# Eleven one-hot lookups in every block, and gathers tied to matmul steps, in a recommendation model's top network

## The chip, the cores and the metric

The kernel runs on one core of a Trainium2 chip. The metric is device time of one execution in microseconds; the median of three runs of the kernel before is 498.77 us (496.91 to 505.03). TensorE (PE) multiplies, VectorE (DVE) and ScalarE (ACT) copy and round, GpSimd (POOL) issues the row gathers, SyncE (SP) issues most other transfers.

## The reference, cut to what matters

```python
e = stack([tbl_f[ids[:, f]] for f in range(26)], axis=1)        # 2048 x 26 x 128, fp32
all_emb = concatenate([bottom[:, None, :], e], axis=1)          # 27 features of 128
gram = einsum('bfd,bgd->bfg', all_emb, all_emb)
h = concatenate([gram[:, triu_i, triu_j], bottom], axis=1)      # 351 + 128
h = maximum(h @ W_top1 + b_top1, 0)                             # 479 -> 512
h = maximum(h @ W_top2 + b_top2, 0)                             # 512 -> 256
y = h @ W_top3                                                  # 256 -> 1
```

Eleven of the 26 tables have 1000 rows (`ONEHOT`). The others have 1250 to 125000.

## The kernel before, in words

The 2048 samples are 16 tiles of 128, in 4 blocks of 4 tiles. An embedding row reaches the matmuls in one of two ways.

**Gather.** POOL issues one indirect transfer for each tile and gathered table (L591): 128 rows land in `rows`, with samples on the partitions. The gathers of a tile come in groups of up to four (`groups_of`), a group fills one of 10 places of the ring `rows`, and POOL waits before a group only until the group ten before it has been transposed. PE transposes a group in one *turn* (`turn(t, g)`, L637, one transpose for each gather), and ACT copies it from PSUM to `features` (L741).

**One-hot lookup.** A *visit* v looks one table up for two blocks (`VISITS`, `lookup(v)`): the table's 1000 rows lie as 8 chunks of 125, and for each chunk and block PE multiplies a high and a low part of the table with a one-hot matrix of 512 samples (L624, L625): 8 x 2 x 2 = 32 matmuls. DVE builds six of the eight one-hot columns (L899) and the low part in two halves (L893), ACT builds columns 2 and 5 (L769, L772) and the high part. Results for block 0 stay in `looked`; those for blocks 1 to 3 go through `staged` to the DRAM tensor `parked` and return, a block at a time, in one transfer of 2.5 to 2.8 MB (`load_looked`, SP, L511). ACT's `place(t)` copies a tile's share into `features`.

`LOOKUPS = (10, 10, 11, 11)` says how many of the eleven small tables are looked up in each block; the rest are gathered. So there are 10 + 11 = 21 visits, and 16 gathers for each tile of blocks 0 and 1 and 15 for each tile of blocks 2 and 3: 8 x 16 + 8 x 15 = 248 gathers in 64 groups (tiles 0 to 7: 4, 4, 4, 4; tiles 8 to 15: 4, 4, 4, 3).

**What follows.** `gram_chunk(t, j)` (L655, four for each tile, 32 matmuls in the trace) makes the products of 32 samples. They go through `products` and `square` in DRAM (SP, `store_products` after a tile's last gram) to `pairs`, and the layers follow for each part of a block (`layer1(part, m)`, `layer2`, `output`).

**The order.** All engines follow one list, `ORDER`, made by `order()`. It keeps a planned time `now` in tenths of a microsecond (`LENGTH`: a lookup 80, a gram 10, a turn 5, a layer-1 column 30, a layer 2 58) and a planned time `gathered` up to which gathers have landed, 13 for each gather. A turn is put in as soon as its rows are planned to be there, no more than four tiles ahead of the grams, and no later than its tile's first gram. PE takes the list strictly in order. Ten visits come first, then block 0's grams with seven visits between them, then block 1's with four; in blocks 2 and 3 there are none. The last stretch of interest here is that of tiles 9 to 13: in the kernel before, `... gram(9,1) turn(12,0) gram(9,2) gram(9,3) gram(10,0) gram(10,1) turn(12,1) layer1(1,0) gram(10,2) layer1(1,1) turn(12,2) gram(10,3) turn(12,3) layer1(1,2) gram(11,0) layer1(1,3) turn(13,0) ...`. SP reaches `load_looked(3)`, the return of block 3's lookups, right after it has stored the products of tile 9, that is after gram(9,3).

Of the kernel before, what the change touches and what calls it, by code (L numbers as in the profile page):

```python
# [18 lines left out]


ONEHOT = [3, 4, 9, 13, 14, 17, 20, 21, 22, 23, 24]
LOOKUPS = (10, 10, 11, 11)
ALWAYS, MOST = min(LOOKUPS), max(LOOKUPS)
ONEHOT_ROWS = 1000
CHUNKS = 8
# [53 lines left out]
TILE_CHUNKS = RUN // CHUNK_GROUPS  # L79
# [27 lines left out]
def groups_of(t):  # L107

    n = TABLES - LOOKUPS[t // BLOCK_TILES]
    return [min(GROUP, n - g) for g in range(0, n, GROUP)]  # L110
# [3 lines left out]
LENGTH = {"lookup": 80, "gram": 10, "layer1": 30, "layer2": 58, "output": 6, "turn": 5, "place": 0, "bottom": 0}  # L114
GATHER_LENGTH = 13
GATHER_START = -20

VISITS = [(i, (b, b + 1)) for b in range(0, BLOCKS, VISIT_BLOCKS) for i in range(LOOKUPS[b])]
FIRST_LATER = LOOKUPS[0]
AMONG = (7, MOST - 7, 0, 0)
# [56 lines left out]
def order():  # L180

    turns = [("turn", t, g) for t in range(TILES) for g in range(len(groups_of(t)))]
    steps, now, gathered = [], 0, GATHER_START
    grams = 0

    def turn():
        nonlocal now, gathered
        step = turns.pop(0)
        gathered += groups_of(step[1])[step[2]] * GATHER_LENGTH
        now = max(now, gathered) + LENGTH["turn"]  # L190
        steps.append(step)

    def rows_are_there():
        t, g = turns[0][1:]
        return t < grams // TILE_CHUNKS + FEATURE_RING and gathered + groups_of(t)[g] * GATHER_LENGTH <= now

    for step in products_and_others():
        if LENGTH[step[0]] and turns and rows_are_there():
            turn()
        while step[0] == "gram" and turns and turns[0][1] <= step[1]:  # L200
            turn()
        steps.append(step)
        now += LENGTH[step[0]]
        grams += step[0] == "gram"
    return steps


ORDER = order()


def accumulations():
# [17 lines left out]
def visited(v):  # L229

    return FILL["lookup", v, VISITS[v][1][-1]] + 1
# [37 lines left out]
def dlrm_tower(nc, xT, ids, onehot_ids, gathered, onehot_tables, w1, b1, w2, b2, w3, square,  # L269
               parked, out):  # L270
    with ExitStack() as ctx:
# [53 lines left out]
        gram = psum("gram", [P, GRAM_RING, BANK])  # L325
# [24 lines left out]
        grammed = sem("grammed")  # L350
        onehot_used = sem("onehot_used")
        accumulated = sem("accumulated")
# [89 lines left out]
        def at_least(eng, semaphore, count):  # L442
            if count > 0:
                eng.wait_ge(semaphore, count)
# [128 lines left out]
        def _(pool):  # L573
# [6 lines left out]
            pool.wait_ge(identity_zero, 1)  # L580
            pool.affine_select(out=identity[:], in_=identity[:], compare_op=ALU.not_equal, fill=1.0,
                               base=0, pattern=[[-1, P]], channel_multiplier=1).then_inc(identity_ready, 1)
            for t in range(TILES):
                if t in (0, FIRST_TILES):
                    pool.wait_ge(index_landed[0 if t == 0 else 1], 16)
                for g, size in enumerate(groups_of(t)):
                    n = groups_before(t) + g
                    at_least(pool, transposed, n - ROWS_RING + 1)
                    for i in range(size):
                        f = GROUP * g + i  # L590
                        pool.indirect_dma_start(  # L591
                            out=rows[:, n % ROWS_RING, i, :], out_offset=None, in_=gathered[f],
                            in_offset=bass.IndirectOffsetOnAxis(ap=index[:, t, f:f + 1], axis=0),
                        ).then_inc(rows_landed[n % ROWS_RING], 16)
# [140 lines left out]
        def _(act):  # L735
# [60 lines left out]
            def place_first(last):  # L796

                at = LOOKED_AT[VISITS[last][0]]
                act.wait_ge(acc_out, FILL["lookup", last - 1, 0] + 1)
                copy_place(0, MOST - LOOKUPS[0], at).then_inc(placed_ahead, 1)  # L800
                looked_up(last, 0)
# [260 lines left out]
```

## Time and profile before

| | us |
|---|---|
| median of three runs | 498.77 |
| lowest, highest | 496.91, 505.03 |
| span of the profiled execution | 370.7 |
| busy in it: PE, DVE, ACT, POOL | 343.2, 236.3, 230.8, 257.2 |

The span runs from the first to the last instruction of the program on the engines. The median is 128 us above it; that part lies around the program, and nothing in the trace shows it. Matmuls overlap, so the pitch from one start to the next is what a matmul costs, not its duration.

### The profile page before, as it was taken

To read this page: it belongs to the slowest core of one execution; us is meant where nothing else is said; L and a number is where in the kernel's file an instruction comes from. 1 tells how busy PE (TensorE), PEld (TensorE's weight loads), DVE (VectorE), ACT (ScalarE), POOL (GpSimd) and SP (SyncE) were. 2 spreads that over 40 slices of the span, in tenths; PEclk is the share of its full clock that TensorE was granted. 3 is DMA by queue.
4 is the path that set the end of the run, shared out by engine and by line. 5 is a ranking of instruction groups with operands and counts; after the bars stand their busy time and mean duration, and the time that the engine had idled before them with its cause. 6 is when DMAs were issued, how large, how long until landed. Compare 5 with 4: busy or idle time off the path is not lost.

```text
span 370.7 us, 8525 instructions
## 1 busy us (share of the span) xinstructions
PE 343.2 (93%) x3422; PEld 282.3 (76%) x3422; DVE 236.3 (64%) x312; ACT 230.8 (62%) x298; POOL 257.2 (69%) x261
## 2 busy tenths in 40 slices
PE   6899999999699999999999999997977996899996
PEld 5688888887587778788788877776866785677886
DVE  2999999999497769798789945313340332522452
ACT  2699989888497896499997833447321473223222
POOL 5777878777777777777877877777777777770010
PEclk9699999999699999999999999999896999899999
DMA  6977687665957789988767629534593425323200
GB/s 174 249 217 211 194 248 222 190 198 163 319 112 251 205 242 341 287 235 252 230 156 245 191 77 347 176 96 114 152 366 99 115 74 146 97 52 85 66 20 2
DMA packets 48391, 66.86 MB, mean 180 GB/s; under 512 B 15861, under 2 KB 34847, under 8 KB 47840
## 3 DMA queue, kind: packets, MB, share of 16 engines
q1 hardware_dynamic: 40024, 49.32, 43.9%
q0 software_dynamic: 8064, 16.31, 16.7%
q10 hardware_dynamic: 264, 0.69, 0.6%
q8 instruction: 27, 0.44, 0.5%
q14 instruction: 12, 0.10, 0.1%
HBM read 52.36 MB, written 13.93 MB: 179 GB/s over the span
## 4 chain that ended last, share of the span: by engine, by line
PE 69%; POOL 10%; DMA 6%; ACT 5%; issue 5%; DVE 3%; SPq 1%; ACTq 0%; DVEq 0%
PE acc L624 21%; PE acc L625 21%; POOL rows L591 10%; PE gram L655 9%; PE turned L637 6%; PE acc L660 4%; PE acc L661 4%; PE acc L662 4%; DMA rows<-in_tbl,index 2%; DMA wanted<-in_onehot_ids 2%; DVE onehot L899 2%; ACT features L741 1%; ACT staged L823 1%; ACT h L769 1%; DMA square<-products 1%
## 5 line engine op out<-in xcount | busy, mean ns | idle before, releaser
L591 POOL DMA_INDIRECT rows<-in_tbl,index x248 | 253.9, 1024 | 77.7 <-issue 74.4
L899 DVE TENSOR_SCALAR onehot<-wanted,row_number 125x1029 fp32r<-125x1029 int32 (+3 forms) x137 | 151.0, 1150 | 19.6 <-PE acc L625 13.3
L624 PE MATMUL acc<-onehot,table_hi 125*128 125x512 f32 x336 | 136.6, 407 | 3.1 <-DVE table_lo L893 3.1
L625 PE MATMUL acc<-onehot,table_lo 125*128 125x512 f32 x288 | 115.7, 402 | 0.0
L624 PEld LDWEIGHTS acc<-onehot,table_hi 125*128 125x128 f32 x336 | 64.7, 193 | 17.8 <-DVE table_lo L893 3.3
L655 PEld LDWEIGHTS gram<-features 128*54 128x54 f32 x2048 | 60.6, 136 | 17.6 <-issue 14.6
L655 PE MATMUL gram<-features 128*54 128x52 f32 x2048 | 67.5, 222 | 6.0 <-DVE features L925 3.0
L625 PEld LDWEIGHTS acc<-onehot,table_lo 125*128 125x128 f32 x288 | 55.7, 194 | 12.4
L769 ACT ACTIVATE h<-wanted,row_number 125x1029 f32<-125x1029 int32 x42 | 48.8, 1163 | 23.4 <-PE acc L625 20.3
L637 PE MATMUL turned<-identity,rows 128*128 128x128 f32 x248 | 41.8, 294 | 9.9 <-DMA rows<-in_tbl,index 8.1
L772 ACT ACTIVATE onehot<-h,row_number 125x1029 fp32r<-125x1029 f32 x42 | 48.6, 1157 | 1.4
L741 ACT COPY features<-turned 128x512 f32<-128x512 f32 x64 | 39.3, 628 | 16.2 <-PE turned L637 15.4
L637 PEld LDWEIGHTS turned<-identity,rows 128*128 128x128 f32 x248 | 29.8, 148 | 17.1 <-DMA rows<-in_tbl,index 9.5
L816 ACT ACTIVATE h<-acc,b_sb 128x512 f32<-128x512 f32 (+1 forms) x20 | 12.1, 604 | 47.7 <-PE acc L662 47.7
L729 DVE COPY products<-gram 117x416 f32<-117x416 f32 x32 | 18.8, 587 | 30.1 <-PE gram L655 23.7
L961 DVE CAST onehot<-h 128x512 fp32r<-128x512 f32 (+1 forms) x20 | 8.0, 399 | 45.0 <-ACT h L816 41.9
L893 DVE TENSOR_TENSOR table_lo<-table_raw,table_hi 125x512 fp32r<-125x512 f32 x36 | 24.6, 682 | 1.7 <-ACT table_hi L761 1.7
L660 PE MATMUL acc<-pairs_hi,w_hi 128*128 128x512 f32 (+1 forms) x60 | 22.3, 371 | 3.2 <-DVE pairs_lo L956 3.0
L729 ACT COPY products<-gram 117x416 f32<-117x416 f32 x32 | 16.1, 504 | 14.6 <-PE gram L655 14.1
L761 ACT CAST table_hi<-table_raw 125x1024 fp32r<-125x1024 f32 x18 | 18.9, 1053 | 8.8 <-DMA table_raw<-in_tbl 8.8
L791 ACT COPY features<-looked 128x1408 f32<-128x1408 f32 (+3 forms) x17 | 23.9, 1406 | 0.0
L661 PE MATMUL acc<-pairs_lo,w_hi 128*128 128x512 f32 (+1 forms) x60 | 21.5, 359 | 0.0
(49 smaller groups left out, 285.4 us busy)
## 6 DMA issues: line engine op xcount, KB each, us to landing
wanted<-in_onehot_ids SPq DMA_DIRECT2D x20, 514.5 KB, 6.0
parked<-staged SPq DMA_DIRECT2D x32, 256.0 KB, 4.3
table_raw<-in_tbl SPq DMA_DIRECT2D x17, 448.0 KB
looked<-parked SPq DMA_DIRECT2D x2, 2816.0 KB, 12.4
square<-products SPq DMA_DIRECT2D x62, 84.5 KB
rows<-in_tbl,index POOLq DMA_INDIRECT x248
looked<-parked SPq DMA_DIRECT2D x1, 2560.0 KB, 11.0
pairs<-in_tbl SPq DMA_DIRECT2D x3, 448.0 KB
```

Of the source, the lines that this page charges most:

```text
L591: pool.indirect_dma_start(out=rows[:, n % ROWS_RING, i, :], out_offset=None, in_=gathered[f], in_offset=bass.IndirectOffsetOnAxis(ap=index ...
L624: pe.matmul(to, table_hi[0:ROW_PARTS, v % HIGH_RING, c, :], of, start=(c == 0), stop=False)
L625: last = pe.matmul(to, raw_table(v, low=True)[0:ROW_PARTS, c, :], of, start=False, stop=(c == CHUNKS - 1))
L637: last = pe.transpose(turned[:, n % 2, i, :], rows[:, n % ROWS_RING, i, :], identity[:])
L655: last = pe.matmul(gram[row:row + HELD * SLOTS, n % GRAM_RING, i * WIDE:(i + 1) * WIDE], of.rearrange("d s f -> d (s f)"), of[:, :, 1:SLOT ...
L660: pe.matmul(to, w_hi, x_hi, start=first, stop=False)
L661: pe.matmul(to, w_hi, x_lo, start=False, stop=False)
L729: return copy(products[0:LAST_ROW, t % PRODUCTS_RING, :, :, first:first + CHUNK_GROUPS].rearrange("f s g t -> f (s g) t"), gram[0:LAST_ROW ...
L741: nc.scalar.copy(features[:, t % FEATURE_RING, :, 1 + GROUP * g:1 + GROUP * g + size, :].rearrange("d u f e -> d f u e"), turned[:, n % 2, ...
L769: nc.scalar.activation(near, ids_of(v, slice(0, ROW_PARTS)), ACT.Abs, bias=row_number[0:ROW_PARTS, CHUNKS + 1 + c:CHUNKS + 2 + c]).then_in ...
L772: nc.scalar.activation(onehot[0:ROW_PARTS, columns_of(v, c)], near, ACT.Relu, scale=-1.0, bias=row_number[0:ROW_PARTS, CHUNKS:CHUNKS + 1]) ...
L899: return dve.tensor_scalar(column[:, rows], ids_of(v, slice(0, ROW_PARTS))[:, rows], row_number[0:ROW_PARTS, c:c + 1], None, ALU.is_equal)
```

## The change

`LOOKUPS` becomes (11, 11, 11, 11): the eleventh small table is looked up for blocks 0 and 1 too. That makes 22 visits (eleven ahead of the first gram) and 15 gathers for each tile: 240 gathers, still in 64 groups, each tile's 4, 4, 4, 3. And POOL waits before each group for a step of PE, which `order()` picks: the last lookup or gram that is planned to end 100 units (10 us) or more before the group is planned to begin.

```diff
-LOOKUPS = (10, 10, 11, 11)
+LOOKUPS = (11, 11, 11, 11)
 ALWAYS, MOST = min(LOOKUPS), max(LOOKUPS)
...
 GATHER_START = -20
+GATHER_LANDS = 38
+PACE_LEAD = 100
...
     steps, now, gathered = [], 0, GATHER_START
     grams = 0
+    begins, ended, paces = [], [], []
 
     def turn():
         nonlocal now, gathered
         step = turns.pop(0)
+        begins.append(gathered - GATHER_LANDS)
         gathered += groups_of(step[1])[step[2]] * GATHER_LENGTH
...
         now += LENGTH[step[0]]
         grams += step[0] == "gram"
-    return steps
-ORDER = order()
+        if step[0] in ("lookup", "gram"):
+            ended.append((now, step))
+    for begin in begins:
+        paces.append(max(((end, step) for end, step in ended if end <= begin - PACE_LEAD), default=(0, None))[1])
+    return steps, paces
+ORDER, PACES = order()
...
+            def keep_pace(n):
+                if PACES[n] is None:
+                    return
+                kind, x, y = PACES[n]
+                if kind == "lookup":
+                    pool.wait_ge(accumulated, visited(x))
+                else:
+                    pool.wait_ge(grammed, x * TILE_CHUNKS + y + 1)
...
                 for g, size in enumerate(groups_of(t)):
                     n = groups_before(t) + g
                     at_least(pool, transposed, n - ROWS_RING + 1)
+                    keep_pace(n)
                     for i in range(size):
```

The list changes with it. Worked out from `order()`, the stretch of tiles 8 to 13 now reads `gram(8,2) turn(11,3) gram(8,3) turn(12,0) gram(9,0) turn(12,1) gram(9,1) turn(12,2) gram(9,2) turn(12,3) gram(9,3) turn(13,0) gram(10,0) turn(13,1) gram(10,1) layer1(1,0) gram(10,2) turn(13,2) layer1(1,1) ...`. From `gram(10,1)` on the turns stand one or two at a time between the other steps. SP still reaches `load_looked(3)` right after the stores of tile 9. Turn (2,2) now stands ahead of gram(0,0) instead of behind it.

The steps that the groups are held to are, for example: group 5 (tile 1, g 1) to lookup 0, group 23 (5, 3) to gram(0,1), group 40 (10, 0) to gram(4,0), group 53 (13, 1) to gram(7,1), group 58 (14, 2) to gram(10,2), group 63 (15, 3) to gram(12,0).

## Rows read from the trace of the kernel before

**Rows 1.** The page: busy time of the engines, and PE's granted clock.

```profile
PE 343.2 (93%) x3422; PEld 282.3 (76%) x3422; DVE 236.3 (64%) x312; ACT 230.8 (62%) x298; POOL 257.2 (69%) x261
...
PEclk9699999999699999999999999999896999899999
```

**Rows 2.** Waits: engine, line, releaser; us in total, times, longest.

```profile
PE turned L637 <- DMA rows<-in_tbl,index: 8.1, 5, 3.7
```

**Rows 3.** Line 591 alone: ns min/median/max, first and last start in us.

```profile
L591 POOL DMA_INDIRECT rows<-in_tbl,index x248: 943/947/1568, 4.1 to 332.3; - x124
```

**Rows 4.** Timeline of POOL: start, duration; gathers 166, 196, 200 and 219.

```profile
229.19 0.94 POOL L591 DMA_INDIRECT rows<-in_tbl,index  x1 [0.30 <-issue]
...
266.71 0.99 POOL L591 DMA_INDIRECT rows<-in_tbl,index  x1 [0.30 <-issue]
...
271.75 0.94 POOL L591 DMA_INDIRECT rows<-in_tbl,index  x1 [0.30 <-issue]
...
295.51 0.95 POOL L591 DMA_INDIRECT rows<-in_tbl,index  x1 [0.30 <-issue]
```

**Rows 5.** Timeline of DVE: the same low half of two visits in a row.

```profile
83.80 0.68 DVE L893 TENSOR_TENSOR table_lo<-table_raw,table_hi 125x512 fp32r<-125x512 f32 x1
...
91.78 0.68 DVE L893 TENSOR_TENSOR table_lo<-table_raw,table_hi 125x512 fp32r<-125x512 f32 x1
```

**Rows 6.** Timeline of PE: the first turn, the first gram, then turns and grams of blocks 1 and 2.

```profile
20.87 0.60 PE L637 MATMUL turned<-identity,rows 128*128 128x128 f32 x4
...
95.73 1.74 PE L655 MATMUL gram<-features 128*54 128x52 f32 x32 [3.02 <-DVE features L925]
...
221.35 0.65 PE L637 MATMUL turned<-identity,rows 128*128 128x128 f32 x4
221.93 1.04 PE L655 MATMUL gram<-features 128*54 128x52 f32 x32
...
228.39 0.49 PE L637 MATMUL turned<-identity,rows 128*128 128x128 f32 x3
228.81 1.04 PE L655 MATMUL gram<-features 128*54 128x52 f32 x32
...
256.14 1.07 PE L655 MATMUL gram<-features 128*54 128x52 f32 x32
...
264.85 3.59 PE L655 MATMUL gram<-features 128*54 128x52 f32 x128
269.49 0.66 PE L637 MATMUL turned<-identity,rows 128*128 128x128 f32 x4 [1.05 <-DMA rows<-in_tbl,index]
```

**Rows 7.** Timeline of PE, on from there: gram(10,2), layer1(1,1), turn(12,2), gram(11,0).

```profile
272.85 1.05 PE L655 MATMUL gram<-features 128*54 128x52 f32 x32
273.83 0.50 PE L660 MATMUL acc<-bottom_hi,w_hi 128*128 128x512 f32 x1
...
280.58 1.11 PE L637 MATMUL turned<-identity,rows 128*128 128x128 f32 x4 [3.70 <-DMA rows<-in_tbl,index]
...
287.91 1.04 PE L655 MATMUL gram<-features 128*54 128x52 f32 x32
```

**Rows 8.** Line 511 and SP's timeline: the returns of looked-up blocks 2 and 3.

```profile
DMA to landing us min/median/max: 11.0/11.2/13.6
...
223.74 0.39 SPq L511 DMA_DIRECT2D looked<-parked  x1
...
269.04 0.34 SPq L511 DMA_DIRECT2D looked<-parked  x1
```

**Rows 9.** Timeline of PE: the turn whose rows were issued during block 2's return.

```profile
237.81 0.66 PE L637 MATMUL turned<-identity,rows 128*128 128x128 f32 x4 [0.62 <-DMA rows<-in_tbl,index]
```

**Rows 10.** Timeline of PE: waits for ACT behind bunched turns of tiles 14 and 15.

```profile
321.10 0.52 PE L637 MATMUL turned<-identity,rows 128*128 128x128 f32 x3 [0.26 <-ACT features L741]
322.20 1.03 PE L655 MATMUL gram<-features 128*54 128x52 f32 x32 [0.58 <-ACT features L741]
...
343.38 1.04 PE L655 MATMUL gram<-features 128*54 128x52 f32 x32 [0.91 <-ACT features L741]
```

## The prediction

> **What bounds the kernel now.** I read the page first. PE is busy 93% of the span, and its granted clock is down only in a few slices [rows 1]. So PE is the bound, and what it waits for must be found by name. The table of waits names the stall that this change touches: 8.1 us in five waits of a turn for gathered rows [rows 2]. The timeline of PE then shows where: at 237.81 (0.62 us), at 269.49 (1.05) and at 280.58 (3.70), all after the visits end at about 220 [rows 6, 7, 9]; the two that are not shown lie at 259.6 and 264.3 and make up the rest. Up to 221 PE waits for no rows at all.
>
> The timeline of POOL is the third view. The gathers follow each other without a break, the first starting at 4.1 and the last ending at 333.3 us [rows 3]. Gather 200 starts at 271.75 and gather 219 at 295.51: 23.76 / 19 = 1.25 us apiece [rows 4]. 248 of them at 1.25 are 310 us. The trace has 329.2, so 19.2 us went into slow ones (up to 1568 ns against a median of 947 [rows 3]), over 21 visits 0.9 us each. The reader is to see two streams: one of rows, at a fixed rate, and one of PE's steps, which is slower than the rows while there are visits and faster afterwards. The rows' lead melts from 221 on, and PE has none left from about 257.
>
> The transfers are the fourth view. Block 3's lookups return in a load issued at 269.04 which takes 11.2 us and so lands at 280.2 [rows 8]. The rows of turn (12,2), gathers 197 to 200, were issued meanwhile, the last by 271.75 + 0.94 = 272.7 [rows 4], and PE got them only at 280.58 [rows 7], 0.3 us after that load. Without a load in the way, the rows of turn (12,1), gathers 193 to 196, were issued by 267.70 [rows 4] and used at 269.49 [rows 6]: 1.8 us. The same happened with block 2's return, issued at 223.74 and landed at 237.3 (13.6 us): the rows of turn (10,1), issued by 230.1 (gather 166), arrived for 237.81 [rows 4, 8, 9]. So rows issued inside such a load land with its end.
>
> **The change, part by part.**
>
> *One more visit.* In the first stretch DVE works without a gap and sets the pace: from one visit's low half to the next are 91.78 - 83.80 = 7.98 us [rows 5], and gram(0,0) waits 3.02 us for DVE's features [rows 6]. The eleventh visit stands in this stretch, so the first gram starts 7.98 us later. What it loads besides (a table, its ids, one more parked result) lies under this. Turn (2,2) moves into PE's wait ahead of gram(0,0): a turn of four is 221.93 - 221.35 = 0.58 us [rows 6], saved.
>
> *Eight gathers less.* A turn of three is 228.81 - 228.39 = 0.42 us, 0.16 less than one of four [rows 6]. Six of the eight shortened turns lie behind the first stretch: 0.96 us less PE time. Turn (9,0), at 221.35 before, comes at 221.35 + 7.98 - 0.58 - 0.96 = 227.8. POOL has 8 x 1.25 = 10 us less to issue, and about 0.9 more from the slow gathers of the 22nd visit: the last one ends at 333.3 - 10 + 0.9 = 324.2. This moves the end only if the rows bound it.
>
> *Where the rows' lead runs out now.* From turn (9,0) to the end of gram(8,2) are 257.1 - 221.35 = 35.8 us, without the row waits (0.62, and 0.07 not shown) 35.1 [rows 6]. In the new kernel gram(8,2) thus ends at 262.9. Up to the end of gram(9,3) follow five turns and five grams (two turns of three at 0.42, three of four at 0.58, the grams at 0.98, which is 273.83 - 272.85 [rows 7]): 7.5 us. So gram(9,3) ends at 270.4. None of these turns waits: the last takes gathers 193 to 195, issued by 266.4 + 0.9 = 267.3 (one pitch before gather 196) and landed 1.8 us later, at 269.1, and it is due at 269.0. The next, turn (13,0), takes gathers 196 to 199; those are issued by 272.4 and land at 274.2 or later. Then comes turn (13,1), due at 270.4 + 0.58 + 0.98 = 272.0 if nothing stood in its way. It takes gathers 200 to 203. Before, these were issued from 271.75 to 276.45 (three pitches and 0.94 on) [rows 4]; now they are issued by 277.4. The new list puts both turns earlier against the grams than the old one did, because its plan lets the rows come as early as PE's steps, and they do not.
>
> *The collision.* SP issues block 3's return after gram(9,3), before at 269.04, with that gram ended at about 264.85 + 2 x 0.9 = 266.65 [rows 6, 8]: 2.4 us later. Now it goes out at 272.8, lands at 272.8 + 11.2 = 284.0, and gathers 200 to 203 lie inside it. Their rows arrive 0.3 us after it, at 284.3, and there PE starts turn (13,1).
>
> *From there to the end.* Before, from turn (12,2) at 280.58 to the end of the span were 90.1 us. This holds the cold start after the stall: from 280.58 to 287.91 are 7.33 us for a turn, a gram, a short turn and a layer-1 column, which at full clock are 0.58 + 0.98 + 0.42 + 2.95 = 4.93 (2.95: from the turn at 269.49 to the gram at 272.85 are 3.36, of which the turn takes 0.41): 2.4 us [rows 6, 7]. The page's row of the granted clock has its dips there and at the first gram [rows 1]. I take the same cost again, though the wait is longer. Left to do after turn (13,1) starts are two layer-1 columns more (5.9) and two grams more (1.96) than before, and three turns less (1.58): +6.3. The turns of tiles 14 and 15 are no longer bunched, so the waits for ACT of 0.26, 0.58 and 0.91 go [rows 10]: -1.75. That leaves 94.7 us, and the span is 284.3 + 94.7 = 379.0 against 370.7: +8.3 us.
>
> *The hold.* It costs nothing where its step is over before POOL gets there. Early that is so by far: group 5 begins with gather 20, at 4.1 + 19 x 1.25 = 27.9 or later, and lookup 0, which it is held to, ends where the first turn starts, at 20.87 [rows 3, 6]. Group 53 begins at 272.7 and is held to gram(7,1), which ends before gram(8,2) does, at 262.9. The tightest are the groups behind the stall. Group 58 starts with gather 219, at 295.51 + 0.9 = 296.4, and is held to gram(10,2), which ends at 284.3 + 1.7 + 4.1 + 1.0 = 291.1 (a cold gram as the first one in rows 6, a column of 2.95 with part of the cold cost, a gram) [rows 4, 6, 7]. The slack is 5.3 us. The cover that makes the hold free is thus POOL's own rate; without it each microsecond of hold would move all later rows by one, and those rows have some 8 us before PE needs them. What a wait that is already met costs POOL shows in the ones it has: the gathers that head a group come at 1.25 us like the others [rows 4]. I take 0 for 59 more. At the outside each costs one gap between gathers, 0.30 us, which is 18 us; but group heads already carry one such wait at an unchanged pitch, and that excludes it.
>
> **A rule against the row.** Twice the trace has rows arriving with the end of the big load, 7.7 and 7.9 us after their issue instead of 1.8 [rows 4, 7, 8, 9]. The Trainium skill, in "DMA: Bandwidth & Descriptors", section "Queues, rings and completion order", has each DMA engine take turns between the queues it has work for, packet by packet. By that rule alone the rows would wait for little more than their own doubled time. The sum by it is the second case below. The sum above goes by the rows.
>
> **The rivals.**
>
> *A, the forecast:* turn (13,1) waits for rows until block 3's return has landed. Span +8.3, time 498.8 + 8.3 = 507.1.
>
> *B, the rows pass the load.* They are used 1.8 to 3.6 us after their issue, at 279.2 to 281.0, and the span is 373.9 to 375.7: 502.0 to 503.8. For it: the rows of turn (12,1) took 1.8 us with stores and a smaller load about [rows 4, 6]. Against it: both loads that a wait of PE touches [rows 7, 8, 9]. This is also what follows by the packet rule.
>
> *C, no row wait at all*, the faster side: the eight saved gathers keep the rows ahead. Turn (13,1) starts at 272.0 and the clock does not fall, so the span is 272.0 + 94.7 - 2.4 = 364.3, -6.4: 492.4. It decides if gather 203 is issued by 270.2, and the trace has it at 276.45 [rows 4]. That would need a third of the 19.2 us of slow gathers to vanish with one more visit. If gathers alone set the end, it would be -9.1, 489.7; but PE's order, not the last gather, ends the span.
>
> *D, the load is as slow as block 2's*, the slower side: 13.6 us instead of 11.2 [rows 8]. PE gets the rows 2.4 us later: 509.5, and 512 if the colder clock costs again what it did. It passes 2% from a load of 12.9 us on. For it: now more rows are in flight beside it. Against it: two of the three loads took 11.0 and 11.2.
>
> *E, the hold bites*: PE's steps are more than 5.3 us later than worked out, and above some 13 us every microsecond counts. Nothing in the trace points to it.
>
> **How the numbers follow.** A 0.50, B 0.20, C 0.07, D 0.18, E and others 0.05. I predict 507.1. The runs of before spread from 496.9 to 505.0, so about 2%, 10 us, is what a measurement can tell from no change; slower by that is above 508.7. A's own terms are good to about 3 us, so a quarter of it lies above; with most of D and E that makes 0.32. Faster takes C's extreme alone, 0.04. Within 2% is left with 0.64. The range must hold most of A, B and D: 499.5 to 512.
>
> **What would show it.** In the new trace: 32 more matmuls and 8 transposes less; the first gram 8 us later; no wait for rows before about 269; one long wait of turn (13,1), up to 12 us with that of (13,0), which ends with `looked` landing at about 284; the last gather near 324; POOL never idle ahead of a group. Wrong would be: a first gram by less than 7 us later, rows used within 3 us of their issue while that load runs, or POOL waiting for L624, L625 or L655. If POOL does wait, the plan's times and the chip's differ more than I read, and E is the case.

## The result, and the profile after

The changed kernel takes 475.15 us (469.02 to 479.69, four runs), the kernel before 498.17 us (496.91 to 505.03, four runs). The ratio is 0.941, with a 95% interval of 0.929 to 0.953. It compares the fast runs alone, on the changed side those of 469.02 and 472.11 us; the medians of all runs stand at 0.954. The change is faster by 5 to 6%, where 507.1 us had been predicted.

The page of the changed kernel, its head (busy us, share of the span, instructions; then PE's granted clock in 40 slices of the span):

```profile
span 466.8 us, 8652 instructions
PE 390.0 (84%) x3446; PEld 309.3 (66%) x3446; DVE 244.7 (52%) x321; ACT 238.1 (51%) x305; POOL 248.6 (53%) x253
...
PEclk9885999999798889899888998799979899699999
```

It does not look like a neighbour of the profile that the prediction was made from. That one had PE busy 93% of 370.7 us [rows 1]. This one has PE busy 84% of 466.8 us, 96 us more span for 24 more matmuls. And this execution took 469.02 us: its span is 2.2 us below its time, not 128 us. The "part around the program" of which the section on the profile before speaks does not exist.

What the engines waited for in the changed kernel (engine, line, releaser; us in total, times, longest; "issue" is time in which the engine waited for nothing that the profile shows, "remote" the update of a semaphore with no instruction beside it that sent it):

```profile
POOL rows L611 <- PE turned L657: 64.8, 17, 8.5
...
PEld gram L675 <- issue: 60.3, 117, 3.6
PE gram L675 <- issue: 37.3, 64, 2.7
POOL rows L611 <- remote: 22.0, 13, 2.5
...
POOL rows L611 <- PE acc L645: 6.7, 1, 6.7
...
POOL rows L611 <- PE gram L675: 3.3, 1, 3.3
```

PE waits for gathered rows nowhere [rows 2]. POOL, whose gathers followed each other at one pitch before [rows 3, 4], now waits 64.8 us for free places of the ring and 10.0 us for the steps of the hold, besides 22.0 us under "remote". The first gram, at 95.73 before [rows 6], starts at 122.72, still behind a wait for DVE's features:

```profile
122.72 1.74 PE L675 MATMUL gram<-features 128*54 128x52 f32 x32 [3.40 <-DVE features L945]
```

### The profile page after: what moved, and what is told of

Its sections match the earlier page's. It is cut to its first block, busy times and chain, and to the rows that moved or that the text cites. A ratio compares the mean times of both kernels' runs of the same rounds, so it can differ in the third digit from the quotient of the medians.

```text
span 466.8 us, 8652 instructions
## 1 busy us (share of the span) xinstructions
PE 390.0 (84%) x3446; PEld 309.3 (66%) x3446; DVE 244.7 (52%) x321; ACT 238.1 (51%) x305; POOL 248.6 (53%) x253
## 4 chain that ended last, share of the span: by engine, by line
PE 78%; issue 11%; another core or an unknown queue 3%; DMA 3%; DVE 3%; SPq 1%; ACT 1%; DVEq 0%
PE acc L645 19%; PE acc L644 19%; PE gram L675 17%; PE turned L657 8%; PE acc L680 5%; PE acc L681 5%; PE acc L682 5%; DVE onehot L919 2%; DMA wanted<-in_onehot_ids 2%; PE acc L721 1%; DMA pairs<-square 1%; SPq L472 1%; DMA square<-products 0%; ACT staged L843 0%
## 5 line engine op out<-in xcount | busy, mean ns | idle before, releaser
L611 POOL DMA_INDIRECT rows<-in_tbl,index x240 | 245.4, 1022 | 162.8 <-PE turned L657 64.8
L919 DVE TENSOR_SCALAR onehot<-wanted,row_number 125x1029 fp32r<-125x1029 int32 (+3 forms) x144 | 158.6, 1147 | 48.4 <-PE acc L645 23.3
L644 PE MATMUL acc<-onehot,table_hi 125*128 125x512 f32 x352 | 151.6, 431 | 21.8 <-DVE onehot L919 13.2
L645 PE MATMUL acc<-onehot,table_lo 125*128 125x512 f32 x304 | 129.0, 424 | 0.1
L675 PE MATMUL gram<-features 128*54 128x52 f32 x2048 | 86.9, 228 | 41.0 <-issue 37.3
L675 PEld LDWEIGHTS gram<-features 128*54 128x54 f32 x2048 | 71.4, 141 | 60.9 <-issue 60.3
L644 PEld LDWEIGHTS acc<-onehot,table_hi 125*128 125x128 f32 x352 | 72.1, 205 | 42.6 <-issue 14.6
L645 PEld LDWEIGHTS acc<-onehot,table_lo 125*128 125x128 f32 x304 | 63.1, 208 | 16.4 <-issue 2.6
L657 PEld LDWEIGHTS turned<-identity,rows 128*128 128x128 f32 x240 | 30.4, 155 | 13.1 <-issue 7.1
L807 ACT COPY staged<-acc 128x512 f32<-128x512 f32 x33 | 18.3, 586 | 13.8 <-PE acc L645 11.5
L811 ACT COPY features<-looked 128x1408 f32<-128x1408 f32 (+2 forms) x17 | 24.4, 1437 | 0.0
```

What stands on the lines that cost most here:

```text
L611: pool.indirect_dma_start(out=rows[:, n % ROWS_RING, i, :], out_offset=None, in_=gathered[f], in_offset=bass.IndirectOffsetOnAxis(ap=index ...
L644: pe.matmul(to, table_hi[0:ROW_PARTS, v % HIGH_RING, c, :], of, start=(c == 0), stop=False)
L645: last = pe.matmul(to, raw_table(v, low=True)[0:ROW_PARTS, c, :], of, start=False, stop=(c == CHUNKS - 1))
L657: last = pe.transpose(turned[:, n % 2, i, :], rows[:, n % ROWS_RING, i, :], identity[:])
L675: last = pe.matmul(gram[row:row + HELD * SLOTS, n % GRAM_RING, i * WIDE:(i + 1) * WIDE], of.rearrange("d s f -> d (s f)"), of[:, :, 1:SLOT ...
L919: return dve.tensor_scalar(column[:, rows], ids_of(v, slice(0, ROW_PARTS))[:, rows], row_number[0:ROW_PARTS, c:c + 1], None, ALU.is_equal)
```

## The experiments

**The kernel before, once more.** The first question was what a profile of the unchanged kernel looks like when its time is near 499 us. In the same session ran the two halves of the change, the lookups without the hold and the hold without the lookups, and the whole change with `PACE_LEAD` at 0, which holds the gathers closer to PE's steps.

`e0_before` has no edit. `e1_lookups` is the changed kernel with

```diff
-                    keep_pace(n)
+                    pass
```

`e2_pace` is the changed kernel with

```diff
-LOOKUPS = (11, 11, 11, 11)
+LOOKUPS = (10, 10, 11, 11)
```

and `e3_lead0` is the changed kernel with

```diff
-PACE_LEAD = 100
+PACE_LEAD = 0
```

> The kernel before, unchanged, profiled once more. The first profile of it had a span of 370.7 us, 127 us under its own times (496.9 to 505.0), while the changed kernel's span (466.8) is 2.2 us under its time (469.0). Theory 1 (the first profile caught an execution that is not like the timed ones): the new span is 495 to 503 us, and PE has well over 60 us of idle time that no semaphore explains (issue), spread over the stretch in which gathers run. Theory 2 (127 us lie around the program in this kernel, and the change took some of that away): the span is 370 us again.

> The changed kernel without the hold: eleven lookups in all blocks, POOL waits for nothing but the ring of rows. Theory 1 (the hold gives the gain, by keeping gathers from running ahead while PE is late): 495 to 508 us, ratio to before 0.99 to 1.02. Theory 2 (fewer gathers and the new order give the gain): 470 to 480 us, ratio about 0.95.

> The kernel before with the hold alone: lookups (10, 10, 11, 11), order as before, the same 10 us lead. Theory 1 (the hold gives the gain): 470 to 482 us, ratio 0.94 to 0.97. Theory 2 (fewer gathers and the new order): 493 to 503 us, ratio 0.99 to 1.01.

> The changed kernel with a lead of 0 instead of 10 us, so each group of gathers is held to a later step. If spreading the gathers over PE's steps is what helps, and rows still come in time: 460 to 472 us. If the lead of 10 us is just what rows need: waits of turns for rows appear and the time is 475 us or more. Theory 2 (the hold does nothing): 475 us, as the changed kernel.

| | us | range | span of the profiled run |
|---|---|---|---|
| before, timed beside them (13 runs) | 504.18 | 499.35 to 507.49, one at 559.77 | |
| unchanged, profiled | 499.71 | one run | 497.9 |
| lookups alone | 506.24 | 499.86 to 510.76 | 497.9 |
| hold alone | 474.4 | 462.44 to 479.7 | 473.5 |
| changed, lead 0 | 467.8 | 453.38 to 473.8 | 471.9 |

The lookups alone give a ratio of 1.0075 (1.0023 to 1.0127). The hold alone gives 474.4/504.18 = 0.941 and the whole change with the closer hold 0.928, by the medians and without an interval (by the medians the whole change had 0.954). The four runs of each scatter over 11 to 20 us, so the three can't be ranked among themselves, but every one of the twelve runs with a hold lies below every run without one. So the gain is the hold's, and the lookups cost a little.

The unchanged kernel's profile, span 497.9 us, is the one that belongs to the time of 499 us. Its waits:

```profile
POOL rows L591 <- PE turned L637: 98.3, 23, 8.1
...
PEld gram L655 <- issue: 63.0, 124, 3.1
PE gram L655 <- issue: 40.5, 75, 1.2
```

In the profile of 370.7 us the same two lines of grams read 14.6 us and 0.8 us:

```profile
PEld gram L655 <- issue: 14.6, 48, 3.2
...
PE gram L655 <- issue: 0.8, 1, 0.8
```

The timeline of PE in the profile of 497.9 us shows how such time lies: a gram is 32 matmuls in one unbroken run in [rows 6], here it breaks into pieces with a gap before each.

```profile
168.18 0.55 PE L655 MATMUL gram<-features 128*54 128x52 f32 x12 [1.19 <-issue]
168.66 0.66 PE L637 MATMUL turned<-identity,rows 128*128 128x128 f32 x4
169.25 1.03 PE L655 MATMUL gram<-features 128*54 128x52 f32 x26
170.70 0.35 PE L655 MATMUL gram<-features 128*54 128x52 f32 x5 [0.42 <-issue]
171.46 0.23 PE L655 MATMUL gram<-features 128*54 128x52 f32 x1 [0.42 <-issue]
172.23 0.63 PE L637 MATMUL turned<-identity,rows 128*128 128x128 f32 x4 [0.54 <-issue]
```

The profile names no semaphore for these gaps. Added up over PE, those above 0.3 us are 53.6 us in 77 places in this profile, 51.4 us in 70 in the changed kernel's, and 0.8 us in one place in that of 370.7 us. Of the 77, 59 (34.4 us) stand ahead of matmuls that wait for no semaphore at all. The other 18 (19.2 us) stand ahead of matmuls that do wait for one, whose update the trace did not record; the longest gap, 7.15 us, ends 0.06 us after the end of the copy of ACT that it waits for.

**Two levels.** The next kernels ran at four later times, called sessions here. The unchanged kernel, timed beside them, took 374.54 us (372.17 to 376.67, 19 runs), 374.19 (370.97 to 377.23, 7), 374.46 (369.74 to 376.72, 25) and 504.87 (494.54 to 506.53, 7). Within a session it stays at its level. Two chips took part: one showed about 504 us in the first session and 374 in the third, the other 374 in the second and fourth and 505 in the fifth. So the level belongs neither to the kernel nor to one of the chips. I call them the 374 level and the 500 level. The profile that the prediction rests on is of the 374 level, the times beside it and the result are of the 500 level.

**The change and its lookups at the 374 level.** `f1_changed` has no edit against the changed kernel, `f2_lookups` is `e1_lookups` again.

> The changed kernel, to be timed where the kernel before takes either about 500 us or about 374 us; both have been seen (the runs of the first experiments took 499 to 507, those of the second 372 to 377, each on one chip). Theory 2 levels (the hold helps only where PE's instructions come late, and the working of the prediction holds where they don't): if before takes 374, this takes 379 to 384, turn(13,1) waits 8 to 12 us for rows, and the ratio is 1.013 to 1.025; if before takes 500, it takes 470 to 480. Rival (the change gains at both levels): at 374 it takes 355 to 370.

> The changed kernel without the hold. Theory 2 levels: if before takes 374, the same as the changed kernel within 0.5%, 379 to 384; if before takes 500, 1.00 to 1.01 of it as before. Rival: the hold matters at both levels, so this is slower than the changed kernel by over 2%.

Measured beside 374.19 us: the changed kernel 383.76 us (382.61 to 385.15, four runs), ratio 1.028 (1.019 to 1.037), span 381.7; without the hold 384.26 us, ratio 1.0275 (1.019 to 1.036), span 383.2. At this level the change is slower, by 9.6 us in the medians, and the hold does nothing. The waits for rows and for PE's steps in the changed kernel there:

```profile
PE turned L657 <- DMA rows<-in_tbl,index: 13.5, 4, 8.9
...
POOL rows L611 <- PE acc L645: 0.9, 3, 0.3
POOL rows L611 <- PE gram L675: 0.3, 1, 0.3
```

**The hold in pieces at the 374 level.** `g1_hold_only` is `e2_pace` again; `g2_hold_lead0` is that with `PACE_LEAD = 0`. `e5_hold_early` holds only groups 0 to 19, `e6_hold_late` (again as `g4_hold_late`) only the groups from 20 on, both in the hold-alone kernel:

```diff
-                if PACES[n] is None:
+                if PACES[n] is None or n >= 20:
```

(`n < 20` in the other two.)

> The kernel before with the hold for gather groups 0 to 19 alone (tiles 0 to 4, the stretch of the first lookups). The profile of before has its largest single loss there: turn(0,3) starts at 84 us instead of 45 to 62. Theory 1a (most of the gain is this one stall): 475 to 483 us, ratio 0.945 to 0.96. Theory 1b (the hold helps all along): 487 to 493 us.

> The kernel before with the hold for groups 20 to 63 alone. Theory 1a: 495 to 505 us, ratio 0.985 to 1.005. Theory 1b: 485 to 493 us, ratio 0.965 to 0.985.

> The kernel before with the hold alone (lead 10 us). At the level of 374: 372 to 376 us, ratio 0.995 to 1.005, since POOL is later than every step that it waits for. At the level of 500: 462 to 480 us, as in the first experiments. Rival: at 374 the waits themselves cost POOL time and rows come later, 377 us or more.

> The kernel before with the hold and a lead of 0. At the level of 374 the steps still end some 5 us ahead of POOL: 372 to 378 us. At the level of 500: 455 to 472 us, better than a lead of 10 us. Rival: at 374 the tighter hold makes rows late, over 380 us.

> The kernel before with the hold for groups 20 to 63 alone. At the level of 374: 372 to 376 us. At the level of 500: theory 1a (the early stall of about 40 us is most of the gain) 493 to 505 us; theory 1b (the hold helps all along) 480 to 492 us.

Measured: early part 0.994 (0.990 to 0.999); late part 1.000 (0.996 to 1.004) and again 1.004 (1.000 to 1.009); whole hold 0.997 (0.993 to 1.002); whole hold with lead 0 1.0075 (1.003 to 1.012). At this level the hold moves the time by less than 1%, and with lead 0 it costs 0.75%. The waits of POOL with lead 0:

```profile
POOL rows L611 <- PE gram L675: 4.3, 7, 2.4
```

The two halves ask which part of the hold brings the gain. They ran at the 374 level, where there is none to divide, so that question stays untested.

**Gathers slowed on purpose.** If issuing gathers less densely is what helps, spacing them should too. `e7_spaced` (again as `f4_spaced`) is the kernel before with POOL filling a scratch tile after each gather:

```diff
+        scratch = sb("scratch", [P, 224])
...
+                        scratches += 1
+                        at_least(pool, scratched, scratches - 1)
+                        pool.memset(scratch[:], 0.0).then_inc(scratched, 1)
```

> The kernel before, no hold, but POOL clears a small scratch after each gather, which stretches the gathers' pitch from 1.25 us to some 1.6 us and leaves a pause between two of them. Theory A (what hurts is gathers issued back to back, at any time): 465 to 485 us. Theory B (what hurts is how many gathers are in flight or ahead of PE, and pauses don't matter): within 1% of before, or slower where rows come late.

> The kernel before with a scratch cleared after each gather. At the level of 374 it took 405 us, since rows then come late. At the level of 500: theory A (back-to-back gathers do the harm) 465 to 485 us; theory B (pauses between gathers don't help) 495 to 520 us.

Measured, both at the 374 level: 405.2 us, ratio 1.082 (1.074 to 1.089), and 405.19 us, 1.085 (1.074 to 1.097). The gathers now last too long and PE waits for rows, in `e7_spaced`:

```profile
PE turned L643 <- DMA rows<-in_tbl,index: 33.0, 12, 9.6
```

This says nothing of the 500 level, where spacing was not tried. At the 374 level it shows what late rows cost: 25 us more waiting [rows 2] and 31 us more time.

**Nearly no gathers.** This run tells whether the 130 us between the levels hang on the gathers. It is the changed kernel, but only the first ten groups, 40 gathers, are issued; later turns transpose what the ring then holds. The other 200 gathers are left out, so the features of most tiles are those of other samples, and the time is that of a kernel without that work. All of PE's, DVE's and ACT's work stays.

```diff
-            return 16 * sum(sizes[m] for m in range(n % ROWS_RING, n + 1, ROWS_RING))
+            return 16 * GROUP
...
-                    at_least(pool, transposed, n - ROWS_RING + 1)
+                    if n >= ROWS_RING:
+                        continue
...
-                    for i in range(size):
-                        f = GROUP * g + i
+                    for i in range(GROUP):
+                        f = min(GROUP * g + i, NG - 1)
```

> The changed kernel with only the first ten groups gathered (40 gathers); all later turns transpose the rows that lie there, so the gathered features are wrong from tile 2 on and PE's work is the same. Theory 1 (PE's instructions come late only while gathers are being issued): PE's idle time that no semaphore explains goes away after about 60 us, the stretch from the first gram on is as in the first profile of before or shorter, and the time is 370 to 400 us. Theory 2 (PE's instructions come late whenever grams run, gathers or not): 440 to 465 us.

> The changed kernel with only the first 40 gathers; the rows transposed later are the old ones, so the gathered features are wrong from tile 2 on. At the level of 374 it took 362. At the level of 500: theory 1 (instructions come late only while gathers are issued) 385 to 410 us, with nearly all unexplained idle time ahead of 70 us; theory 2 (they come late whenever grams run) 440 to 465 us.

> The changed kernel with only the first 40 gathers; gathered features are wrong from tile 2 on. At the level of 374: 361 to 364 us again. At the level of 500: theory 1 (instructions and loads come late only while gathers are issued) 385 to 410 us; theory 2 (they come late whenever grams run) 440 to 465 us.

> The changed kernel with only the first 40 gathers; gathered features are wrong from tile 2 on. At the level of 374: 361 to 364 us once more. At the level of 500: theory 1 (instructions and loads come late only while gathers are issued) 385 to 410 us; theory 2 (they come late whenever grams run) 440 to 465 us.

Measured at the 374 level: 361.92 us (0.966, 0.959 to 0.974), 363.25 (0.973, 0.963 to 0.983) and 362.96 (one run). At the 500 level, beside a kernel before of 504.87 us: 381.28 us, one run, span 379.3. So the same removal that saves 384 - 363 = 21 us at one level saves 475 - 381 = 94 us at the other (the 475 is from another session; the nearest kernel beside the 381, `h1_early_return` below, took 480.99). The levels, 130 us apart for the kernel before, are 18 us apart for this one. Its gathers and its grams at the 500 level (for the first line: ns min/median/max, first and last start in us):

```profile
L612 POOL DMA_INDIRECT rows<-in_tbl,index x40: 940/944/1457, 4.0 to 61.6; - x40
```

```profile
PEld gram L676 <- issue: 15.6, 53, 3.2
...
PE gram L676 <- issue: 0.8, 1, 0.8
```

The unexplained gaps of the grams are gone, to the figures of the 374 level. And the 18 us lie ahead of the first gram, the stretch in which it still gathers: from the first gram to the end it takes 379.3 - 123.8 = 255.5 us, the same kernel at the 374 level 360.7 - 103.7 = 257.0.

The same by windows of four profiles: the kernel before at the 374 and at the 500 level, the changed kernel at the 500 level, the one with few gathers at the 500 level (window; length, then busy us and instructions of PE, PEld, DVE, ACT, POOL; granted clock, DMA share, GB/s):

```profile
20.00:70.00 50.00, 50.00 (x231) 40.76 (x230) 50.00 (x57) 44.59 (x52) 39.84 (x34) 1.00 0.74 211
130.00:330.00 200.00, 185.87 (x2306) 150.91 (x2305) 110.44 (x149) 116.73 (x156) 152.92 (x155) 0.97 0.62 188
```

```profile
20.00:70.00 50.00, 20.23 (x74) 14.85 (x73) 13.43 (x15) 11.46 (x14) 34.83 (x37) 0.68 0.37 100
130.00:330.00 200.00, 163.19 (x1392) 123.95 (x1391) 109.76 (x123) 106.73 (x134) 117.70 (x119) 0.91 0.56 172
```

```profile
20.00:70.00 50.00, 37.49 (x150) 28.88 (x149) 32.08 (x36) 30.09 (x35) 34.18 (x32) 0.86 0.54 148
130.00:330.00 200.00, 168.41 (x1427) 129.99 (x1426) 107.74 (x120) 107.61 (x134) 113.60 (x118) 0.91 0.54 164
```

```profile
20.00:70.00 50.00, 34.46 (x133) 26.45 (x132) 30.39 (x35) 25.72 (x30) 27.87 (x28) 0.80 0.49 142
130.00:330.00 200.00, 196.08 (x2437) 160.37 (x2436) 126.02 (x164) 137.53 (x180) 0.00 (x0) 1.00 0.51 156
```

In the first window the kernel before issues 230 matmuls at one level and 74 at the other, with POOL doing nearly the same number of gathers (34 and 37) and the DMA engines busy 37% of the time, at 100 GB/s where the other level moves 211. The loss is thus no lack of bandwidth. In the second window the kernel without gathers keeps PE busy for 196 of 200 us, the two that gather for 163 and 168. (Its count of matmuls, 2437 against some 1400, says less, since the others are then at earlier steps with larger matmuls.)

**An earlier return.** `h1_early_return` is the changed kernel with the load that turn (13,1) waits behind issued after tile 8's stores:

```diff
-                if kind == "layer1" and y == 1 and x + 2 < BLOCKS:
-                    load_looked(x + 2)
+                if kind == "layer1" and y == 1 and x == 0:
+                    load_looked(2)
+                if (kind, x, y) == ("gram", 2 * BLOCK_TILES, TILE_CHUNKS - 1):
+                    load_looked(3)
```

> The changed kernel with block 3's return issued after tile 8's stores instead of tile 9's, so at about 269.5 instead of 278.2 us at the level of 374. Theory (the rows of turn(13,1) come late because that transfer is under way): the transfer lands at about 281, the wait of 8.9 us ahead of turn(13,1) shrinks, turn(13,0) or (12,3) may wait more, turn(13,1) starts at 281 to 284 instead of 288.7, and the time is 376 to 380 instead of 383.8. Rival (the gathers alone are late and the transfer doesn't matter): 383 to 385, as before. At the level of 500 both expect the time of the changed kernel, 470 to 480.

It ran at the 500 level: 480.99 us (474.77 to 482.6, four runs), 0.961 (0.937 to 0.985) of the kernel before beside it. The changed kernel had 0.941, and the two intervals overlap. There PE waits for no rows, so there was nothing for the edit to remove. What it would bring at the 374 level, where turn (13,1) waits 8.9 us, was not measured.

**Where the hold gains at the 500 level.** The stages of eight profiles, from the starts of PE's steps, in us:

| | level | turn (0,0) to (0,3) | first gram | first gram to gram(14,0) | span |
|---|---|---|---|---|---|
| before | 374 | 23.7 | 95.7 | 226.5 | 370.7 |
| changed | 374 | 23.7 | 104.1 | 230.6 | 381.7 |
| before | 500 | 64.4 | 135.1 | 314.3 | 497.9 |
| lookups alone | 500 | 61.4 | 140.6 | 309.6 | 497.9 |
| changed | 500 | 41.3 | 122.7 | 296.5 | 466.8 |
| changed, early return | 500 | 44.1 | 133.3 | 297.9 | 478.5 |
| changed, lead 0 | 500 | 31.7 | 136.0 | 288.6 | 471.9 |
| hold alone | 500 | 42.2 | 128.0 | 286.7 | 473.5 |

From lookups alone to the whole change the span falls by 31.1 us: 17.9 ahead of the first gram, 13.1 from there to gram(14,0). This split is that of two single executions. The early return is the same kernel up to the first gram and reaches it at 133.3, not 122.7, and from before to the hold alone 7.1 us fall ahead of the first gram and 27.6 behind it. So the hold gains in both stretches, 5 to 18 us in the first and 12 to 28 in the second, and no finer. Most of what is lost ahead of the first gram is one stall between turns (0,0) and (0,3). In the kernel before at the 500 level, PE:

```profile
37.91 0.79 PE L624 MATMUL acc<-onehot,table_hi 125*128 125x512 f32 x1 [7.15 <-issue]
...
56.97 0.79 PE L624 MATMUL acc<-onehot,table_hi 125*128 125x512 f32 x1 [12.10 <-DVE onehot L899]
...
67.79 0.77 PE L624 MATMUL acc<-onehot,table_hi 125*128 125x512 f32 x1 [8.75 <-DVE onehot L899]
```

and DVE, which these wait for:

```profile
55.63 1.29 DVE L899 TENSOR_SCALAR onehot<-wanted,row_number 125x1029 fp32r<-125x1029 int32 x1 [19.10 <-remote]
66.75 0.89 DVE L899 TENSOR_SCALAR onehot<-wanted,row_number 125x882 fp32r<-125x882 int32 x2 [9.84 <-remote]
71.76 2.48 DVE L899 TENSOR_SCALAR onehot<-wanted,row_number 125x1029 fp32r<-125x1029 int32 x2 [4.12 <-remote]
```

All this time POOL issues a gather every 1.25 us, until the ring is full. The windows view of all engines (window; length, then busy us and instructions of PE, PEld, DVE, ACT, POOL; granted clock, DMA share, GB/s) and POOL's timeline:

```profile
48.00:55.50 7.50, 0.00 (x0) 0.00 (x0) 0.00 (x0) 0.00 (x0) 5.67 (x7) 0.50 0.19 52
```

```profile
64.86 0.95 POOL L591 DMA_INDIRECT rows<-in_tbl,index  x1 [0.30 <-issue]
72.30 0.95 POOL L591 DMA_INDIRECT rows<-in_tbl,index  x1 [6.50 <-PE turned L637]
```

From turn (0,3) on PE and DVE run as at the 374 level for a while: to turn (1,2) are 23.7 us at both. In the changed kernel the hold stops POOL after 27 gathers, where in the kernel before the ring stops it after 48, and the stall is 23 us shorter:

```profile
38.10 0.94 POOL L611 DMA_INDIRECT rows<-in_tbl,index  x1 [0.30 <-issue]
45.73 1.34 POOL L611 DMA_INDIRECT rows<-in_tbl,index  x1 [6.68 <-PE acc L645]
```

**What comes late is PE's signal.** In the stall PE waits for DVE, and DVE for PE. The semaphore behind DVE's 19.10 us is `onehot_used`, which PE alone raises, when it is done with a one-hot column. The trace also keeps the time of every semaphore update that it recorded. The last matmul that PE had done ended at 44.87, the update came at 55.53, and DVE started at 55.63: the work was done, and its signal came 10.7 us after it. All waits of DVE, ACT and POOL that the profile calls "remote" end with such an update of a semaphore that PE alone raises. They add up to 279 us in this profile, 240 with the lookups alone, 199 in the changed kernel's, 37 with few gathers, and none in the two profiles of the 374 level in the table. Of PE's 321 recorded updates, 98 come more than 1 us after the last matmul that raises their semaphore; at the 374 level none of 345 does. With few gathers it is 11 of 354, the last of them at 43.85 us, and none after the last gather. Late signals come through in bursts when POOL pauses: five between 71.66 and 71.90 in the kernel before, where POOL had stopped at 65.81, six between 42.35 and 42.65 in the changed one, where it had stopped at 39.04. That is the likeliest way in which the hold gains; which pauses are needed was not tested.

## Why the prediction was wrong

**The step that failed** stands in no term of the sum but in its base: "498.8 + 8.3". I took the span of 370.7 us and a time of 498.8 us for one and the same execution, with 128 us around the program. They were executions at two levels, and the span belonged to a time near 374. In the 500 level's profile of the same kernel the span is 497.9 of 499.7 us. The sum was thus made for a kernel bound by PE with POOL never held back, and read off against one in which the engines stand idle on signals of PE that come late while POOL runs ahead. For that one the prediction had no term at all. A span a quarter below the median should have been the first thing to doubt.

**The hold at nothing** (rival E, 0.05) fell with it. The sum had +8.3 us for the lookups and 0 for the hold. At the 500 level the lookups alone made 0.75% (0.2 to 1.3%), 2 us in the medians, and from there the hold took 31.1 us off the span. "The cover that makes the hold free is thus POOL's own rate" is right at the 374 level: POOL waits 1.2 us for the hold's steps in all. At the 500 level PE's steps are late by tens of microseconds, so the hold bites, as the prediction's last sentence allowed. But it bites with the opposite sign: a wait on POOL was counted as a loss only, for the rows it delays. What it gives, pauses of POOL while PE is behind, had no place in the sum.

**At the 374 level, most terms of the sum hold**, with a span of 381.7 us against the 379.0 worked out. The changed kernel's PE there:

```profile
104.10 1.05 PE L675 MATMUL gram<-features 128*54 128x52 f32 x32 [3.03 <-DVE features L945]
...
269.57 0.66 PE L657 MATMUL turned<-identity,rows 128*128 128x128 f32 x4 [1.28 <-DMA rows<-in_tbl,index]
...
273.32 0.90 PE L657 MATMUL turned<-identity,rows 128*128 128x128 f32 x3 [2.12 <-DMA rows<-in_tbl,index]
274.15 1.74 PE L675 MATMUL gram<-features 128*54 128x52 f32 x32
277.06 1.12 PE L657 MATMUL turned<-identity,rows 128*128 128x128 f32 x4 [1.17 <-DMA rows<-in_tbl,index]
...
288.73 1.12 PE L657 MATMUL turned<-identity,rows 128*128 128x128 f32 x4 [8.89 <-DMA rows<-in_tbl,index]
```

and its SP and POOL at that place:

```profile
278.20 0.34 SPq L519 DMA_DIRECT2D looked<-parked  x1
```

```profile
269.32 0.95 POOL L611 DMA_INDIRECT rows<-in_tbl,index  x1 [0.31 <-issue]
...
279.52 0.94 POOL L611 DMA_INDIRECT rows<-in_tbl,index  x1 [0.30 <-issue]
```

- *First gram 7.98 us later:* 8.4.
- *The 22nd visit costs the gathers 0.9 us:* 3.8, for the visit and the new order together. Summed over the trace, the gathers' time above 0.945 us each is 23.3 us against 19.5 before. This is the term that was mis-sized. Gather 195 ends at 270.3, not 267.3, and gather 203 at 280.5, not 277.4.
- *None of the turns up to (12,3) waits:* they wait 1.28 and 2.12 us, turn (13,0) 1.17. The rows of (12,2) and (12,3) are the late ones, and they were used 3.0 us after their issue instead of 1.8. gram(9,3) ends near 275.9 instead of 270.4.
- *The load goes out 2.4 us after gram(9,3) and turn (13,1) starts 11.5 us after it:* 2.3 and 10.5. It is the one long wait, 8.89 us, and its rows came 8.3 us after the last of them was issued. Rival B, the rows passing the load, is not what happens. The prediction set a rule of the Trainium skill ("DMA: Bandwidth & Descriptors", "Queues, rings and completion order") on its side, and read too little in it: by that section an engine drains a whole packet, typically 9 to 17 descriptors, from one queue before it changes to the next. The trace has this load in 128 pieces of 22,528 bytes, 8 for each of 16 engines. If a piece is one descriptor, which is an assumption, the load can be a single turn, and the rule agrees with the row. The DMA engines' GB/s in 40 slices of 1.125 us from 255 to 300 show the load from the 21st slice (277.5 us) to the 30th, which ends at 288.75, where the turn starts:

```profile
GB/s 51 29 40 58 60 186 206 106 66 176 178 122 189 241 126 199 82 55 55 26 247 376 189 470 304 451 444 479 251 157 64 73 62 58 58 58 58 69 62 18
```

  Rows that come as the load ends, then. The packets of this trace show them held back meanwhile: from 270 to 277 us the gathers' queue had 182 packets (0.35 MB), from 280 to 287, beside 116 packets (2.47 MB) of the load's queue and with the DMA engines 90% busy, only 70 (0.16 MB), and from 287 to 288 it had 116 (0.25 MB), when 122 of the load's 128 pieces had ended by 287.5 (the last ends at 290.2). What an earlier load would bring was not run at this level.
- *94.7 us from there to the end:* 381.7 - 288.73 = 93.0.
- *Last gather near 324:* 326.9.

The rise at the 374 level, 9.6 us in the medians and 11.0 between the two spans, is near the predicted 8.3, partly since two errors offset each other (turn (13,1) later by 4.4 us, the rest shorter by 1.7).

**What was not settled.** What sets the level is open; what else ran on the chip and where the tensors lay were not looked at. Shown is that the loss is there only with gathers (381.3 us in one run with 40 of them, 468 to 506 in the medians with 240 or 248), that it takes the form of late signals of PE and of gaps in its grams, and that holding POOL back takes part of it away. Open is why gathers delay PE's signals at one level and not at the other. In the 500 level's profile of before, 95% of PE's unexplained idle time begins less than 2 us after a gather's start, and such times make up 70% of the span; but that is only a correlation. For the gaps inside a gram there are two readings, a late supply of instructions and a PE that is held while its own signals don't go out, and no run separates them. The 27 packets of the queue that carries instructions take 1.00 us in the median at either level, so their transfer itself is not what is slow. Which groups the hold must hold at that level was not measured either.

**The best of the kernels** timed at both levels is the hold without the eleventh table: 474.4 us at the 500 level, no worse than the changed kernel's 475.15 by what four runs can tell, and 373.95 us at the 374 level, where the changed kernel takes 383.76. The closer hold was timed with the lookups at one level only (467.8 us at 500) and without them at the other only (0.75% slower than before at 374), so it is not ranked here.

## What to carry to other kernels

Before a sum is made on a profile, lay its span beside the time of its own execution and beside the median: here they differ by 2 us when they belong together, and 128 us of difference meant that the profile answered another question. Time spent under "issue" inside runs of equal instructions (40.5 us against 0.8) is a bottleneck with a size, even though no semaphore names it. Where two engines seem to wait for each other, lay the time of the semaphore's update beside the end of the work that sends it: here 10.7 us lay between them. And a producer that runs ahead of its consumer is not free merely because it has nothing else to do: where it disturbs the others, holding it to the consumer's steps gained about 6% here; where it does not, the hold with a lead of 10 us cost nothing that could be measured, and with none 0.75%.

## What the runs showed of the hardware

- One kernel, unchanged, takes 374 us in some sessions and 504 in others, on either of two chips, with a range of 1 to 2.5% within a session, one run of 559.77 us apart. PE's mean granted clock was 0.880 in its profile of 497.9 us and 0.963 in that of 370.7 us, and in the stalls it falls further (0.68 in the window from 20 to 70 us of the former, 1.00 in the same window at the 374 level). The clock follows the stalls: up to the first gap matmuls come every 0.23 us, and behind the gap of 7.15 us one lasts 0.63 instead of 0.40. So it adds to the loss and does not start it.
- At the 500 level, signals of PE came late while gathers were being issued, at least 18 us late at the most in the kernel before: 98 of 321 updates more than 1 us late, against none of 345 at the 374 level and, with 40 gathers, 11 of 354.
- With one more visit and the new order, the gathers' slow time rose by 3.8 us in all, four times the mean of a visit (0.9) that the trace of before gave.
- With 40 gathers early in the program the levels are 18 us apart. The remaining 200 cost 94 us at the 500 level and 21 us at the 374 level, of which 13.5 are visible waits for rows.
- Rows whose gathers were issued while a load of 2.8 MB was under way came as that load ended, 7.7 to 8.3 us after their issue instead of 1.6 to 3.0.
